# Moving the zero-fills later in each sequence, and reordering the step from expert tiles to shared tiles

## The reference

```
x = x + attention(layernorm(x))        # 16 heads of 128, rotary positions, causal softmax
x = x + ffn(layernorm(x))
ffn(x):
  scores = softmax(x @ gate_w.T)       # 8 experts
  topk_w, topk_idx = top_k(scores, 2); topk_w /= sum(topk_w)
  y_all  = (silu(x @ w1[e]) * (x @ w3[e])) @ w2[e]      # inner width 176, all experts
  y      = sum over the 2 chosen experts of y_all * topk_w
  shared = (silu(x @ sw1) * (x @ sw3)) @ sw2            # inner width 352
  return y + shared
```

## Time and profile before

| | |
|---|---|
| median of three executions | 762.35 us |
| the profiled execution | 762.67 us |
| its span | 760.9 us |
| PE busy | 722.0 us (95%) |
| DVE busy | 646.2 us (85%) |
| ACT busy | 528.7 us (69%) |
| POOL busy | 493.9 us (65%) |
| mean granted TensorE clock | 0.984 of full |
| chain that ended last | PE 79%, DVE 9%, ACT 5%, POOL 2% |

### The profile page before, as it was taken

The page is one execution under the profiler, slowest core; times in us unless marked ns, Lnnn a source line. Parts: engine busy times, 40 slices in busy tenths (PEclk is TensorE's granted clock), DMA queues, the critical chain, the costliest instruction groups (busy, mean ns, idle before and its releaser), DMA issues.

```text
span 760.9 us, 16176 instructions
## 1 busy us (share of the span) xinstructions
PE 722.0 (95%) x5403; PEld 686.6 (90%) x5403; DVE 646.2 (85%) x1831; ACT 528.7 (69%) x1661; POOL 493.9 (65%) x512
## 2 busy tenths in 40 slices
PE   4899999999999999999999999999999797999994
PEld 3787999999999999999999999999999797999993
DVE  6898889988998989898989988998889455788868
ACT  4788777777777777777778777777677732566641
POOL 4778667777778777877777777777757322344420
PEclk9999999999999999999999999999999998899997
DMA  6554203321332143223302321312444603244464
GB/s 203 137 166 139 99 28 110 124 105 35 120 107 95 37 136 125 69 65 130 136 27 90 124 97 41 103 38 92 174 174 160 243 16 97 76 126 134 153 214 168
DMA packets 49338, 85.85 MB, mean 113 GB/s; under 512 B 8424, under 2 KB 40008, under 8 KB 47656
## 3 DMA queue, kind: packets, MB, share of 16 engines
q1 hardware_dynamic: 45208, 73.39, 28.6%
q0 software_dynamic: 4048, 11.42, 4.2%
HBM read 60.07 MB, written 44.59 MB: 138 GB/s over the span
## 4 chain that ended last, share of the span: by engine, by line
PE 79%; DVE 9%; ACT 5%; POOL 2%; issue 2%; DMA 1%; SPq 1%; DVEq 0%; POOLq 0%; ACTq 0%
PE bank L623 61%; PE bank L663 4%; PE bank L656 3%; PE bank L672 3%; DVE work L997 2%; PE bank L844 1%; PE bank L875 1%; PE bank L873 1%; PE bank L863 1%; DVE work L990 1%; ACT work L1383 1%; PE bank L772 1%; DVE w_lo L964 1%; POOL work L467 1%; ACT w_hi L1366 1%
## 5 line engine op out<-in xcount | busy, mean ns | idle before, releaser
L1578 POOL TENSOR_TENSOR qkt_lo<-work,qkt_hi 128x512 fp32r<-128x512 f32 x128 | 166.0, 1297 | 84.1 <-ACT qkt_hi L1376 84.1
L467 POOL TENSOR_TENSOR work<-work 128x512 f32<-128x512 f32 x127 | 165.2, 1301 | 47.6 <-DVE work L997 44.7
L997 DVE TENSOR_TENSOR work<-bank,sinn 64x512 f32<-64x512 f32 x256 | 176.2, 688 | 3.4
L623 PE MATMUL bank<-xnt_hi,w_lo 128*128 128x256 f32 x512 | 146.2, 286 | 2.5 <-POOL w_lo L1642 1.8
L1376 ACT CAST qkt_hi<-work 128x512 fp32r<-128x512 f32 x128 | 79.5, 621 | 96.0 <-POOL work L467 94.3
L623 PE MATMUL bank<-xnt_lo,w_hi 128*128 128x256 f32 x512 | 145.7, 285 | 0.0
L623 PE MATMUL bank<-xnt_hi,w_hi 128*128 128x256 f32 x512 | 145.7, 285 | 0.0
L1383 ACT ACTIVATE work<-work,bias 128x128 f32<-128x128 f32 (+1 forms) x256 | 112.7, 441 | 0.0
L990 DVE TENSOR_TENSOR work<-bank,cosn 128x512 f32<-128x512 f32 x128 | 88.0, 688 | 19.6 <-PE bank L623 19.1
L623 PEld LDWEIGHTS bank<-xnt_hi,w_lo 128*128 128x128 f32 x512 | 98.6, 193 | 3.3 <-DVE xnt_lo L1028 3.2
L623 PEld LDWEIGHTS bank<-xnt_hi,w_hi 128*128 128x128 f32 x512 | 99.0, 193 | 0.0
(11 more groups left out here) (163 smaller groups left out, 2128.9 us busy)
## 6 DMA issues: line engine op xcount, KB each, us to landing
rows_by_expert<-in_zero_t SPq DMA_DIRECT2D x17, 1028.0 KB
weights_split<-stage SPq DMA_DIRECT2D x40, 176.0 KB, 1.9
w_lo<-weights_split SPq DMA_DIRECT2D x4, 1408.0 KB, 9.5
stage<-rows_by_expert SPq DMA_DIRECT2D x39, 128.5 KB, 2.1
w_lo<-results_by_token SPq DMA_DIRECT2D x16, 256.0 KB, 5.1
w_hi<-weights_split SPq DMA_DIRECT2D x2, 1536.0 KB, 6.3
stage<-in_L_ffn_w SPq DMA_DIRECT2D x32, 88.0 KB, 2.2
weights_split<-stage SPq DMA_DIRECT2D x20, 128.0 KB, 1.8
```

Source lines behind the costliest of these rows:

```text
L467: eng.tensor_tensor(roped[:, a], rope_cos[:, a], rope_sin[:, a], ALU.add).then_inc(rope_add, 1)
L623: mm = pe.matmul(out, lhs[a], rhs[b], start=start and n == 0, stop=stop and n == 2, skip_group_check=more)
L997: op = nc.vector.tensor_tensor(rope_sin[lo:lo + 64, a], p_qk[a][hi:hi + 64, :, :], sn, ALU.mult)
L1578: nc.gpsimd.tensor_tensor(qkt[a][1][:, :, :], roped[:, a], qkt[a][0][:, :, :], ALU.subtract).then_inc(qkt_lo, 1)
```

## The change

Two independent edits. The first changes after which pieces SP issues a fill: before, those with k % 5 = 1, 2 and 3; after, those with k % 5 = 2, 3 and 4. The second changes the order of work where the expert tiles end, on PE, DVE and ACT: both `up_s` of shared tile 9 come before `turn_e` of the last expert tile, `down_e` of the last expert tile comes behind both `up_s` of shared tile 10, and ACT's and DVE's steps are reordered to suit.

```
@@ SP
-                if 1 <= k % 5 <= 3 and parts_left:
+                if k % 5 >= 2 and parts_left:
                     clear(*parts_left.pop(0))
@@ PE
-            up_s(S1, 0)
+            for u in range(2):
+                up_s(S1, u)
             turn_e(NJ - 1)
             down_e(NJ - 2, e[NJ - 2])
-            up_s(S1, 1)
-            down_e(NJ - 1, e[NJ - 1])
             for t in range(S1 + 1, NT):
                 for u in range(2):
                     up_s(t, u)
+                if t == S1 + 1:
+                    down_e(NJ - 1, e[NJ - 1])
                 turn_s(t - 1)
@@ DVE
+            rows_low(S1 + 1)
+            mult_s(S1)
             low_e(NJ - 1)
             result(NJ - 2)
-            mult_s(S1)
-            result(NJ - 1)
-            rows_low(S1 + 1)
             for t in range(S1 + 1, NT):
                 if t + 1 < NT:
                     rows_low(t + 1)
                 mult_s(t)
+                if t == S1 + 1:
+                    result(NJ - 1)
                 low_s(t - 1)
@@ ACT
+            rows_high(S1 + 1)
+            silu_s(S1)
             high_e(NJ - 1)
-            silu_s(S1)
             half(NJ - 2)
-            half(NJ - 1)
-            rows_high(S1 + 1)
             for t in range(S1 + 1, NT):
                 if t + 1 < NT:
                     rows_high(t + 1)
                 silu_s(t)
+                if t == S1 + 1:
+                    half(NJ - 1)
                 high_s(t - 1)
```

## The result

| | before | after |
|---|---|---|
| median | 761.81 us (4 executions) | 799.12 us (4 executions, 794.67 to 802.41) |
| ratio to before | | 1.049, 95% interval 1.0434 to 1.0547 |
| profiled execution | 762.67 us | 800.9 us |
| its span | 760.9 us | 799.1 us |
| PE busy | 722.0 us | 733.4 us |

What follows compares the result with a forecast made beforehand. It took PE, busy 449.44 of 450 us between 90 and 540 us, as the bound. 762.67 + 18.5 (five sequences of 3.7) + 0.3 (tail) = 781.5, 781.2 after the 0.3 above the median; range 767 to 790.

Steps and rivals of the forecast that it cites:

- Place and chain of edit 1: Sequences 1 to 5: the new fill delays round 13's scatter, POOL waits in round 14, `low` starts late, PE stands 2.5 us.
- the landing of the scatter: Round 13's scatter beside the moved fill: lands in 6.0 us, bounds 3.2 and 8.2; the term known least.
- its own formula: PE's wait in round 15: landing less 2.5 us, less 0.2 for `low`'s wait for ACT, less PE's margin of 0.8.
- The upper bound of 8.2 us: Longest landing allowed for round 13's scatter, from POOL's store of rows with a fill under way: five times 6.4, 32 us.
- the rows of the prediction: Profile rows of transfers beside a fill: store 8.2 us, weight load 5.6, round 12 scatter 5.8; they priced the landing.
- The Trainium skill's round-robin: DMA engines alternate packets between queue rows, so round 13's scatter, with two or three turns, lands in 5.2 to 6.4 us.
- The clock: After PE's idle time in each of five sequences, a lower clock costs 1.2 us, at most 1.7.
- What was relieved: With the fill behind k % 5 = 1 gone, POOL's round 5 store and some loads land earlier; PE gains nothing.
- 1.5 forecast: Kernel's tail: PE waits 1.5 us before tile 13, behind ACT's wait for that tile's rows.
- +0.3 forecast: Kernel's tail: 1.5 us won before tile 10 goes into waiting for tile 13's rows, net +0.3 us.
- the forecast's bound of +1.9: Kernel's tail: upper bound of the reordering's cost, +1.9 us if the last result's whole delay reaches the end.
- case (c): Rival: round 13's scatter held as long as the store, 8.2 us, clock lost each time: 794.7 us, chance 0.09.

Runs made afterwards that it cites:

- e1: The kernel before with only the fills moved to behind k % 5 = 2, 3, 4, the end as before: 797.9 us, ratio 1.0464.
- e4: The changed kernel with the fills moved in sequence 1 only, those of later sequences at k % 5 = 1, 2, 3 as before: 771.31 us, ratio 1.0125.
- e5: The changed kernel with POOL's wait for the scatters moved behind the subtraction of round 14: 793.61 us, ratio 1.0402.
- e6: The changed kernel with the fills behind k % 5 = 1, 2 and 4: 790.57 us, ratio 1.038.
- e2: The changed kernel with the fills back at k % 5 = 1, 2, 3, so only the end reordered: 763.52 us, ratio 1.0027.

## Why the prediction was wrong

- **Place and chain of edit 1: right.** The fill behind k % 5 = 4 meets the scatter of round 13, POOL's wait in round 14 holds `low`, PE waits at L656, once in each of sequences 1 to 5. e1, e4 and e5 bear this out.
- **The step that failed: the landing of the scatter, "I take 6.0".** It was 9.1 us in sequence 1:

```profile
rows_by_expert<-xn,slot POOLq DMA_INDIRECT x1, 9.1
```

  In sequences 2 to 5 it was 9.5, 9.3, 9.1 and 7.9 us, the last behind the fill of 514 KB; the prediction took five fills of 13.7 us. With 9.1 its own formula gives 9.1 - 2.5 - 0.2 - 0.8 = 5.6 us of PE's wait, five times 28; measured 27.0. The upper bound of 8.2 us was no bound. It came from a store issued 5.6 us into its fill, and the round 12 scatter behind the 6.0 was issued 9 us into one: both were let go about when the fill ran out. The scatter of round 13 had 11.0 us or more of the fill of 13.7 us ahead of it in sequences 1 to 4. The prediction noted that the fill "won't end first" and then took its value from rows where it did.
- **How a scatter is held.** The packets of the two queues in the changed kernel, in stretches of its trace (queue, kind: packets, MB, share of 16 engines), show it. First 166 to 168 us:

```profile
q0 software_dynamic: 36, 0.10, 12.9%
q1 hardware_dynamic: 3, 0.10, 11.4%
```

```profile
q1 hardware_dynamic: 10, 0.33, 26.8%
```

  Then 4 of the scatter follow by 172, 2 by 173, 4 by 174 and 2 by 175. The row of 172 to 173 us, and the row of 175 to 177 us, when the scatter is through and the fill is not:

```profile
q0 software_dynamic: 2, 0.01, 2.0%
```
```profile
q1 hardware_dynamic: 6, 0.07, 7.7%
```

  So the first of the remaining twelve came some 3 us behind the 36, the time of more than two packets of 1.26 us, and the first four were through about 4 us behind them; the other eight came a few at a time, about a packet of the fill apart. That makes 6 us to the first four and 3 more to the last, the 9.1 us of the landing. Only a fill that ends sooner, as in e6 and in the rows of the prediction, cuts it short. The Trainium skill's round-robin, which was weighed in the prediction (DMA: Bandwidth & Descriptors, Queues, rings and completion order) and gave 5.2 to 6.4 us, fits the later turns and leaves out this first wait. Why some three packets of the fill went first is not shown; that they were already queued on the engine is a guess.
- **The clock: right in kind, too small.** Taken were 1.2 us a sequence, from the nearest row, of 3.4 us at a lower clock behind 1.94 us idle. Measured were 11.4 / 5 = 2.3 us. Behind the 5.8 us idle of sequence 1 the lower clock lasted through most of 6.4 us (0.58), with PE busy throughout. What sets its size stays open: e5, with shorter waits (17.5 us in five), had PE busy for 735.1 us, 13.1 more than before, and e4, with one wait of 5.68 us, for 722.9 us, 0.9 more.
- **What was relieved, at nothing: right.** POOL's store of round 5 in sequence 2 lands in 2.4 us instead of 8.2, and PE gains nothing by it.
- **Edit 2: right in its waits, too low in their price.** No wait before tile 10, 1.31 us before tile 13 (1.5 forecast; its own times, 737.0 - 1.5 to 737.3, give 1.8), net 0.0 in the profiled execution (+0.3 forecast). But edit 2 alone is 1.0027, some 2 us slower, which is at the forecast's bound of +1.9; its interval, 1.0009 to 1.0046, reaches beyond it. The prediction counted no clock behind the new wait, which is long enough to lose it in some executions: e2's profile shows it lost, the profile after does not.
- **The chances.** 0.09 stood on case (c), with the long landing and the clock lost each time. It is the one that came, and even its 794.7 us were too few, since it took the store's 8.2 us for the landing and 1.7 us for the clock. The range ended below it, at 790.

The sum with the measured terms: 27.0 (waits) + 11.4 (clock) + 0.0 (end) = 38.4, and 762.67 + 38.4 = 801.1, where the profiled execution took 800.9 us.

## What to carry to other kernels

When a transfer will be issued beside a long one, take as the bound on its landing the time that the long one has left, plus the transfer's own time alone. No store or scatter read here beside a fill was over that; the slowest neighbour in a trace where the long one soon ran out is no bound. For each row taken as a price, read how far into the long transfer it was issued.
